# The order of three jobs in GpSimd's queue: cache rows, new rows and a root of variances in a fused attention and adapter kernel

## What is computed

```python
q = q_proj(x); k = k_proj(x); v = v_proj(x)        # 8 query heads, 4 key heads of 64
q = _rms(q, q_norm_scale); k = _rms(k, k_norm_scale)   # x * rsqrt(mean(x*x) + 1e-6) * (1 + scale)
q = _rope(q, pos); k = _rope(k, pos)
k_blocks = k_blocks.at[blk, :, off, :].set(k)      # new keys and values go into a paged cache
v_blocks = v_blocks.at[blk, :, off, :].set(v)
k_all = k_blocks[block_tables]; v_all = v_blocks[block_tables]
o = softmax(mask(q @ k_all.T / 16)) @ v_all        # a window of 256 positions for each query
x = x + o @ Wo.T
```

## Time and profile before

| | us |
|---|---|
| time, median of 3 runs | 459.12 |
| lowest, highest | 458.86, 460.43 |
| span of the profiled execution | 503.1 |
| PE busy in it | 450.7 (90%) |
| DVE busy | 302.0 (60%) |
| POOL busy | 267.9 (53%) |
| ACT busy | 229.6 (46%) |
| TensorE's granted clock, mean | 0.976 of 2.4 GHz |

### The profile page before, as it was taken

How to read it: one execution, slowest core, us unless ns; L and a number is a source line. 1 busy time by engine, 2 the same in 40 slices (tenths; PEclk the granted TensorE clock), 3 DMA queues, 4 the chain that set the end, 5 groups by cost and what they waited for, 6 DMA issues and landing times.

```text
span 503.1 us, 9985 instructions
## 1 busy us (share of the span) xinstructions
PE 450.7 (90%) x2890; PEld 326.4 (65%) x2890; DVE 302.0 (60%) x869; ACT 229.6 (46%) x590; POOL 267.9 (53%) x241
## 2 busy tenths in 40 slices
PE   5999997799797899898989898999999998979997
PEld 2444467455476677585857676777677766857776
DVE  4988873375464466464756565665656475756542
ACT  1322112343564365454555564555555555555541
POOL 2588166446665546565665656657565655654000
PEclk9999997799998989999999999999999999999999
DMA  6385867837335665545455554645454545444111
GB/s 195 104 303 193 287 186 202 261 99 245 85 110 125 172 166 134 140 105 167 104 154 153 140 166 126 166 123 169 111 166 108 170 108 144 116 138 118 49 55 43
DMA packets 80731, 74.29 MB, mean 148 GB/s; under 512 B 51012, under 2 KB 57284, under 8 KB 80678
## 3 DMA queue, kind: packets, MB, share of 16 engines
q1 hardware_dynamic: 61712, 47.22, 32.6%
q0 software_dynamic: 15456, 22.08, 16.5%
q10 hardware_dynamic: 3510, 4.35, 2.4%
HBM read 83.59 MB, written 11.93 MB: 190 GB/s over the span
## 4 chain that ended last, share of the span: by engine, by line
PE 61%; DVE 9%; issue 8%; SPq 6%; DMA 6%; ACT 5%; another core or an unknown queue 4%; ACTq 0%; DVEq 0%
PE banks L1104 23%; PE banks L1235 7%; PE banks L1241 6%; PE banks L1117 6%; PE banks L1268 5%; PE banks L1253 4%; PE banks L1098 4%; PE banks L1217 2%; DMA mask<-masks_dram 2%; DMA stage<-wo_dram 2%; DVE prob L974 2%; DVE x L892 2%; PE banks L1281 1%; ACT x L667 1%
## 5 line engine op out<-in xcount | busy, mean ns | idle before, releaser
L519 POOL DMA_INDIRECT windows<-kvrows_dram,idx_all x78 | 82.1, 1053 | 64.8 <-PE banks L1253 29.2
L639 ACT ACTIVATE pt_s<-banks 112x384 f32<-112x384 f32 x128 | 57.5, 498 | 88.5 <-PE banks L1241 67.6
L519 POOL DMA_INDIRECT windows<-newkv,idx_all x78 | 78.8, 1011 | 29.4 <-issue 21.9
L633 ACT ACTIVATE prob<-prob,negmax 128x336 f32<-128x336 f32 x128 | 72.2, 565 | 37.9 <-DVE negmax L974 21.5
L974 DVE CUSTOM_DVE_ANT_0 prob<-banks,mask 128x336 f32<-128x336 f32 x128 | 58.6, 505 | 47.7 <-issue 25.8
L489 POOL TENSOR_TENSOR rstd<-ms,half 128x8 f32<-128x8 f32 x24 | 46.3, 1928 | 72.6 <-DVE ms L912 52.3
L1117 PE MATMUL banks<-wkv_s,xt_s 128*128 128x512 f32 x128 | 59.1, 617 | 6.0 <-DMA xt_s<-xt_dram 5.2
L1235 PE MATMUL banks<-kt_s,qt_s 64*128 64x336 f32 x256 | 50.2, 482 | 4.9 <-ACT kt_s L627 3.4
L1241 PE MATMUL banks<-cst,prob 128*112 128x128 f32 x384 | 53.4, 275 | 0.0
L1104 PE MATMUL banks<-wf_hi,x 128*128 128x512 f32 x120 | 42.1, 412 | 10.0 <-DVE x L892 8.6
L984 DVE TENSOR_SCALAR prob<-prob,rinv 128x336 f32<-128x336 f32 x128 | 49.0, 425 | 2.3
(11 more groups left out here) (211 smaller groups left out, 821.3 us busy)
## 6 DMA issues: line engine op xcount, KB each, us to landing
usel<-utab SPq DMA_DIRECT2D x64, 128.0 KB
xt_s<-xt_dram SPq DMA_DIRECT2D x31, 256.0 KB
mask<-masks_dram SPq DMA_DIRECT2D x32, 168.0 KB
newkv<-kvo SPq DMA_DIRECT2D x16, 256.0 KB, 3.5
stage<-xtok_dram SPq DMA_DIRECT2D x16, 256.0 KB
tsel<-ttab SPq DMA_DIRECT2D x64, 64.0 KB
out_dram<-xo ACTq DMA_DIRECT2D x15, 256.0 KB
windows<-kvrows_dram,idx_all POOLq DMA_INDIRECT x78
```

Source lines behind the costliest of these rows:

```text
L519: P.indirect_dma_start(kv_s[i][:, c, :], None, newkv if new else kvrows, bass.IndirectOffsetOnAxis(ap=idx_all[:, new * CH + c, b:b + 1], a ...
L633: A.activation(pr, pr, ACT.Exp, bias=negmax[:, g:g + 1], scale=-1.0, accum_out=psum_p[b % 2][:, g:g + 1]).then_inc(S["exp_done"], 1)
L639: A.activation(pt_s[g][:], tb[g % 2][0:KP, 0:CH * 128].rearrange("p (c q) -> p c q", c=CH), ACT.Copy).then_inc(S["pt_ev"], 1)
```

## The change

In an odd half nothing changes. In an even half the old rows of k + 4, with the wait for `pv_mm` ahead of them, go first, the new rows of k + 2 follow, and the root is last as before. Half 0 is apart and stays. In half 28 there are no old rows left to gather, so its order is what it was. The order differs in the 13 even halves from 2 to 26.

```diff
-                if k + 2 < NB:
-                    gather(k + 2, 1)
+                t = k // 2
+                if k % 2 == 1:
+                    if k + 2 < NB:
+                        gather(k + 2, 1)
+                    if k + 4 < NB:
+                        pool.wait_ge(S["pv_mm"], k)
+                        gather(k + 4, 0)
+                    continue
                 if k + 4 < NB:
                     pool.wait_ge(S["pv_mm"], k)
                     gather(k + 4, 0)
-                if k % 2 == 0 and k // 2 + 1 < TILES:
-                    root_query(k // 2 + 1)
+                if k + 2 < NB:
+                    gather(k + 2, 1)
+                if t + 1 < TILES:
+                    root_query(t + 1)
```

## The result

The changed kernel takes 471.44 us (median of 5 runs, 467.00 to 473.44), the kernel before 458.86 us (455.62 to 460.43): a ratio of 1.0298, 95% interval 1.0254 to 1.0342. It is 3% slower, and the forecast of 459.2 us and its range up to 465.0 were wrong. Some executions of a kernel are a little slower than its others, and the ratios are formed without them, so a ratio is not exactly the quotient of the two medians beside it.

A forecast was written before the change was run, and what follows sets the result against it. The prediction took PE to bound the kernel and GpSimd to set no time. Its terms, old rows, root, new rows, odd half and DVE, each cost zero and summed to 0 us, giving 459.2 us, range 457.2 to 465.0.

The forecast's parts named there:

- What bounds the kernel: Whole kernel: PE busy 90% of the span with 61% of the chain; GpSimd (POOL) busy 53%, no chain entry.
- The old rows gain nothing: GpSimd, even half: old rows still start when `pv_mm` rises; only idle time grows, to about 5.8 us.
- The root: GpSimd's root, even half: ends 9.72 to 9.83 instead of 8.10, still ahead of `qrot`; cost zero, small margin.
- The new rows of k + 2: Even half's moved gathers: land 3.5 us after issue, before `keys_t`; cost zero, 1.6 to 2.0 us to spare.
- a quiet time: At 7 to 9 us, when new rows travel, DMA engines are busy for 0.11, then 0.46 of the time.
- The reader's time: PE's `keys_t`: 12.00 us after the first old-row DMA in half 14, 11.60 in half 22.
- the forecast's own clock: Time counted from the start of half 14's first old-row DMA, at 286.21 in the trace.
- The odd half: GpSimd, odd half: new rows start at 9.9 to 10.0 instead of 8.28; no delay carried on.
- DVE beside the moved DMAs: DVE at 3.91 to 7.48 doesn't hold up GpSimd's moved DMAs: zero; otherwise plus 2 to 3 us.
- The first one, new rows late: Slower rival: PE waits at odd-half `keys_t`, sign "DMA windows<-newkv" before L1217; 4 to 5.6 us, 463 to 465; chance 0.23.
- The second: Slower rival, root late: `qrot` and `queries_t` wait for GpSimd; 2.6 to 5 us less PE's slack, 460.8 to 462; chance 0.13.
- The third: Faster rival: GpSimd close to the bound when not profiled; gain 4 us at most, 455 to 457.5; chance 0.12.

The follow-up runs named there:

- e2_new_first: Kernel before, with even halves' new rows issued behind the wait for `pv_mm` but ahead of the old rows, root last: 458.92 us, ratio 1.0013.
- f8_empty_new: Changed kernel with the moved new-row gathers' bound set to zero, so hardly a row travels: 465.16 us, ratio to before 1.0185, two executions.
- h3_small_usel: Changed kernel with SP's `usel` loads alone cut to an eighth from the third tile on: 458.83 us, ratio to before 1.002.
- h1_after: The changed kernel once more, unaltered, as yardstick beside `h3_small_usel`: 468.07 us against 458.06 for the kernel before, ratio 1.025.
- after: The changed kernel itself in its first measurement against the kernel before: 471.44 us, ratio 1.0298.
- e4_small_tsel: Changed kernel with SP's `tsel` loads cut to a quarter from the third tile on: 472.27 us, ratio to before 1.0248.
- e3_new_last: Kernel before with even halves reordered to old rows, root, then new rows behind both: 562.49 us, ratio 1.2243.
- e1_before: The kernel before, unchanged, run again for a second trace: 457.58 against 458.05 us, ratio 0.9995, profiled span 455.4 us.

## Why the prediction was wrong

**What bounds the kernel** was read rightly: PE, with GpSimd off the path.

**The old rows gain nothing**: right. GpSimd is idle for 3.5 to 5.1 us ahead of them in the changed kernel (12.2 once, behind the late mask), and nothing starts earlier.

**The root**: right in its result. It starts right behind the last DMA, and `qrot` follows 0.96 us after its end in the half shown. The forecast had 0.2 to 0.7 us; the root took 1.68 us and not 2.04, and started 0.03 behind the DMA and not 0.19. `e2_new_first` shows the cost of the late root alone: none that can be measured.

**The new rows of k + 2**: this step failed, and in it the landing time. The prediction had the bounds 1.9, 3.5 and 5.6 us from issue to landing and took 3.5, the middle row, a 256 KB load of SP. Measured was 5.76 us in the half shown and 5.4 to 6.5 in all that wait, mostly beyond the upper one, which was the only one of the same kind, an indirect DMA of GpSimd. The row of the same kind was the nearest; size was a poor guide, as `f8_empty_new` shows, where hardly any bytes travel and the time stays. What sets it is the `usel` loads on SP's queue (`h3_small_usel`: 1.9 to 2.3 us after the end of the issue, with them 4.2 to 5.7). The earlier trace rows were read as a quiet time; a share that is the mean of 16 engines did not show that about two of them had a load on them for 13 us and more.

The Trainium skill, DMA: Bandwidth & Descriptors, section Queues, rings and completion order, says that each DMA engine serves its queues in turn, a packet of each. By that rule a small gather waits for packets of SP's load on the same engines, which fits the runs: where `usel`'s packets travel, two at a time, a few of a gather's landing records come late, and where they don't, none does. The lengths of the packets, 0.16 us against 0.013, would account for why `tsel` does no harm. In which order an engine takes the queues, no trace here shows.

**The reader's time** was a second, smaller error in the same step. It was read from a trace in which a tile took 23.74 us. In the runs that were timed it takes 20.66, and `keys_t` comes 11.68 us after the first old-row DMA, within 0.1 us in every even half from batch 8 on, where the prediction had 12.00 in half of them. The prediction saw that the timed runs were 44 us shorter and said that the margins would shrink, but put no number on it. With the landing alone mended, the forecast's own clock gives 6.50 + 5.76 = 12.26 against 12.00 and 11.60, so 0.3 to 0.7 us a half, some 6 us in 13. With both numbers mended it is: landing at 268.43 - 261.95 + 5.76 = 12.24 after the first old-row DMA, `keys_t` wanted at 11.68, so 0.6 us a half, 7 us in 13 halves. Measured were 10.3 us of stalls; 1.4 us of the difference belong to one half, where GpSimd needed 2.42 us between two issues instead of 0.30, and two more halves had the landing 0.7 us later than the half shown:

```profile
308.17 0.99 POOL L519 DMA_INDIRECT windows<-kvrows_dram,idx_all  x1 [2.42 <-issue]
```

**The odd half** and **DVE beside the moved DMAs**: right in their result. The moved DMAs took 0.99 us each, all 39 of them, and no `keys_t` of an odd batch waits. The reading behind it had a gap: it says that DVE works on PSUM operands and reductions in that time and leaves out L914, which adds two SBUF tiles and starts at 292.08, 5.87 on the prediction's clock. In the changed kernel the same addition (L922, 267.52) runs beside the second moved DMA, which takes its 0.99 us all the same.

**The rivals.** The first one, new rows late, was what happened, by its own mechanism and its own sign; its price of 4 to 5.6 us was half of the real one. It had been given a chance of 0.23. The second did not happen. The third had its premise right (a tile is 3 us shorter) but GpSimd's idle time covered it.

## What to carry to other kernels

When a DMA is moved closer to its reader, take the landing time from DMAs of the same kind by the same engine, and weigh what other queues load at that moment; bytes say little for a small gather, and neither does the mean busy share of the DMA engines when a load sits on two of them. Check that the trace's span is near the time that is measured (here 503 against 459 us) before margins of half a microsecond are read from it. Where two queues' loads collide, moving the one with slack can be worth more than the order of the other: `usel` in the odd half brought 2.5% here.

## What the runs showed of the hardware

- SP's `usel` loads, four of 128 KB, each into 32 partitions, delay the landing of a small indirect gather from some 2.2 us to 4.2 to 5.7 us after the end of its issue (`h3_small_usel` against `h1_after` and `after`); `tsel`, four of 64 KB, don't (`e4_small_tsel`).
- These `usel` loads travel mostly two packets at a time and take 13 to 16 us for 512 KB; of the 48 landing records of a gather's three DMAs 4 to 7 come late beside them.
- After 6.5 us without work TensorE's granted clock was 0.50 for at least 4 us, and work that takes 0.79 us took 1.38 (`e3_new_last`). In the changed kernel, with stalls of 0.2 to 2.0 us, it stayed near full, 0.989 on average against 0.993 in `e1_before`; behind the longest stall it was 0.50 for 3.4 us (from 318.9), after a stretch of 2.9 us in which PE was busy for 0.68 us.
- GpSimd's `rstd` on 128x8 takes 2.05 us where it had waited for its operand, and 1.68 where it stood directly behind a DMA:

```profile
L489 POOL TENSOR_TENSOR rstd<-ms,half x24: 1637/1676/2156, 21.4 to 420.5; 128x8 f32<-128x8 f32 x24
```

The median of the same line was 2042 ns before.
